# W_up of all experts in one transfer, one low half on GpSimd, and scale two tiles behind, in a conditional adapter kernel on one core

## The reference

```python
h = x @ W_down[e] + b_down[e]        # 512 -> 256
h = gelu(h)                          # exact
h = h @ W_up[e] + b_up[e]            # 256 -> 512
h = x + h
h = (h - mean(h)) * rsqrt(var(h) + 1e-5)
out = h * ln_w[e] + ln_b[e]
```

## Time and profile before

| | |
|---|---|
| time, median of 3 runs | 139.28 us (139.13 to 139.84) |
| profiled execution | 138.9 us, its span 137.1 us |
| PE busy | 126.5 us, 92% of the span |
| DVE busy | 112.4 us, 82% |
| POOL busy | 103.6 us, 76% |
| ACT busy | 84.7 us, 62% |
| TensorE clock granted, mean | 0.992 |
| DMA | 21.94 MB, mean 160 GB/s |

### The profile page before, as it was taken

How to read it: one execution, slowest core, us unless ns; L and a number is a source line. 1 busy time by engine, 2 the same in 40 slices (tenths; PEclk the granted TensorE clock), 3 DMA queues, 4 the chain that set the end, 5 groups by cost and what they waited for, 6 DMA issues and landing times.

```text
span 137.1 us, 4074 instructions
## 1 busy us (share of the span) xinstructions
PE 126.5 (92%) x846; PEld 112.7 (82%) x847; DVE 112.4 (82%) x275; ACT 84.7 (62%) x176; POOL 103.6 (76%) x117
## 2 busy tenths in 40 slices
PE   6969799999979999999999999999999999999830
PEld 6868688878969999999999999999999999998610
DVE  1889669868969979888988897889788978897992
ACT  0587569526696666666676666666666666666600
POOL 7002595567589988888888888888888898889860
PEclk9999999999999999999999999999999999999996
DMA  1964999996463355454444455545546633331355
GB/s 41 329 216 145 268 272 309 292 261 196 143 180 94 116 153 153 155 155 153 153 155 153 153 155 153 153 153 153 153 153 153 153 77 77 81 77 38 86 160 180
DMA packets 13200, 21.94 MB, mean 160 GB/s; under 512 B 2297, under 2 KB 3842, under 8 KB 13186
## 3 DMA queue, kind: packets, MB, share of 16 engines
q1 hardware_dynamic: 8802, 15.74, 40.6%
q10 hardware_dynamic: 4384, 6.05, 14.6%
HBM read 13.39 MB, written 8.65 MB: 161 GB/s over the span
## 4 chain that ended last, share of the span: by engine, by line
PE 67%; DVE 11%; DMA 6%; issue 4%; ACTq 3%; ACT 3%; POOL 3%; DVEq 2%; POOLq 0%
PE hg_ps L896 29%; PE y_ps L924 26%; PE xT_ps L882 8%; DMA wd<-in_L_cond_W_down_dram 4%; PE hg_ps L905 4%; DMA x_sb<-in_x_dram 2%; DVE r_stats L706 2%; DVE hb L694 2%; POOL res L386 2%; DVE xT_lo L686 1%; DVE scaled L727 1%; DVE res L742 1%; DVE gT_lo L700 1%; DVE wu_lo L260 1%; ACTq L457 1%
## 5 line engine op out<-in xcount | busy, mean ns | idle before, releaser
L369 POOL TENSOR_TENSOR xb<-x_sb,bu_rows 128x512 f32<-128x512 f32 x33 | 42.9, 1301 | 11.3 <-DVE bu_rows L681 9.8
L386 POOL TENSOR_TENSOR res<-normed,lnb_rows 128x512 f32<-128x512 f32 x31 | 39.8, 1285 | 12.1 <-ACT normed L488 12.1
L468 ACT ACTIVATE g<-hb 128x256 f32<-128x256 f32 x33 | 13.8, 418 | 35.9 <-DVE hb L694 35.9
L706 DVE BATCH_NORM_STATS2 r_stats<-y_ps 128x6 f32<-128x512 f32 x33 | 22.9, 695 | 7.4 <-issue 7.0
L924 PE MATMUL y_ps<-wu_hi,gT_hi 128*128 x66 | 23.3, 434 | 1.5 <-ACT gT_hi L473 1.4
L896 PE MATMUL hg_ps<-wd_hi,xT_hi 128*128 x132 | 23.8, 302 | 0.9 <-issue 0.8
L686 DVE TENSOR_TENSOR xT_lo<-xT_ps,xT_hi 128x512 fp32r<-128x512 f32 x33 | 22.8, 691 | 1.3 <-ACT xT_hi L463 1.1
L727 DVE SCALAR_TENSOR_TENSOR scaled<-y_ps,r_mv,lnw_rows 128x512 f32<-128x512 f32 x31 | 22.9, 743 | 0.4 <-DMA lnw_rows<-in_L_cond_ln_w_dram 0.4
L375 POOL TENSOR_TENSOR rstd<-var_eps,half_neg 128x1 f32<-128x1 f32 x33 | 18.2, 551 | 5.9 <-DVE var_eps L715 5.8
L488 ACT ACTIVATE normed<-scaled,rstd 128x512 f32<-128x512 f32 x31 | 22.3, 723 | 0.0
L896 PE MATMUL hg_ps<-wd_lo,xT_hi 128*128 x132 | 21.1, 282 | 0.0
(11 more groups left out here) (88 smaller groups left out, 146.8 us busy)
## 6 DMA issues: line engine op xcount, KB each, us to landing
x_sb<-in_x_dram SPq DMA_DIRECT2D x64, 128.0 KB, 2.9
out_dram<-res ACTq DMA_DIRECT2D x33, 128.0 KB, 2.5
out_dram<-res SPq DMA_DIRECT2D x33, 128.0 KB, 2.5
wd<-in_L_cond_W_down_dram ACTq DMA_DIRECT2D x3, 512.0 KB, 5.6
wu<-in_L_cond_W_up_dram SPq DMA_DIRECT2D x3, 512.0 KB, 5.5
lnw_rows<-in_L_cond_ln_w_dram SPq DMA_DIRECT2D x1, 768.0 KB, 9.0
lnb_rows<-in_L_cond_ln_b_dram SPq DMA_DIRECT2D x1, 768.0 KB, 11.0
x_sb<-in_x_dram ACTq DMA_DIRECT2D x2, 128.0 KB, 2.9
```

The source lines that it names most:

```text
L369: pool.tensor_tensor(xb[:, c % DEEP, :], x_sb[:, c % FAR, :], bu_rows[:, ds(e * H, H)], ALU.add).then_inc(xb_ready, 1)
L386: pool.tensor_tensor(res[:, c % FAR, :], normed[:, c % DEEP, :], lnb_rows[:, ds(e * H, H)], ALU.add).then_inc(res_ready, 1)
L706: dve.bn_stats(r_stats[:, c % DEEP, :], y_ps[c % YBANKS][:]).then_inc(stats_ready, 1)
```

## The change

- **Loads.** One static transfer of 1,536 KB holds W_up of all three experts. SP issues it behind the first halves of tiles 0 and 1, and before anything that needs the second part of the tables. The load of 12 registers (L305) is gone; tiles 2 to 6 load their two registers each with `entries` (L276). x of tile 5 now goes behind ln_w.
- **Slots.** wu now lies by expert. ACT, DVE and POOL each load three registers (`wu_from`) that say which expert a slot has, and slice `wu` by them. ACT waits once for the whole transfer.
- **ACT's start.** In tile 0 `gelu(0)` and `seed(1)` now come ahead of `wu_high(0)`.
- **Low halves.** Slots 0 and 1 stay on DVE; slot 2 goes to POOL, behind `add_bias(3)` and ahead of `power(0)`.
- **up.** In tiles 0 to 2 the product with `gT_lo` comes second and that with `wu_lo` last.
- **Distances.** `LATE = 10`: on DVE `scale` runs two tiles behind in 3 to 9, with the catch-up `scale(8)` at the end of 9; on ACT `rescale` runs four behind in 4 to 10, with the catch-up `rescale(7)` at the end of 10, and x_hi(6), which followed x_hi(5) in tile 4, comes in tile 5; on POOL `shift` runs two behind up to tile 9. PE transposes two tiles ahead in 2 to 5, with x of tile 8 as the extra one in tile 5 (before: x of tile 6 in tile 3). The loops start at 6 (PE), 10 (DVE, POOL) and 11 (ACT).

```diff
-        def load_w_up(eng, slot, e):
-            eng.dma_start(wu[:, slot, :, :], w_up[ds(e, 1), :, :].rearrange("a (c p) n -> p (a c) n", p=P)).then_inc(
-                wu_in[slot], 16)
+        def load_w_up(eng):
+            eng.dma_start(wu[:].rearrange("p e c n -> p (e c) n"), w_up.rearrange("e (c p) n -> p (e c) n", p=P)).then_inc(
+                wu_in, 16)
...
+        def w_up_part(source):
+            return wu[:].rearrange("p e c n -> p (e c n)")[:, ds(source * (KB * H), KB * H)]
+
+        def w_up_sources(eng, regs):
+            eng.reg_load(regs, wu_from[0:1, 0:E])
+            return [eng.snap(reg, min_val=0, max_val=E - 1 - slot) + slot for slot, reg in enumerate(regs)]
...
-            sp.wait_ge(slots_ready, 2)
-            sp.reg_load(next_regs, io_table[0:1, 5:17])
-            for t in range(2, 6):
-                if t < 2 + E:
-                    slot = t - 2
-                    load_w_up(sp, slot, sp.snap(next_regs[3 * slot], min_val=0, max_val=E - 1 - slot) + slot)
-                load(t, t, [sp.snap(reg, min_val=0, max_val=B - 1) for reg in next_regs[3 * t - 5:3 * t - 3]])
+            load_w_up(sp)
+            for t in range(2, 5):
+                load(t, t, entries(t, 0, 2))
             sp.dma_start(lnw_rows[:], rows_of(ln_w, P)).then_inc(lnw_in, 16)
-            load(6, 6, entries(6, 0, 2))
+            for t in range(5, 7):
+                load(t, t, entries(t, 0, 2))
...
+            w_up_low(pool, 2, w_up_sources(pool, pool_regs)[2]).then_inc(wu_lo_last, 1)
+            for t in range(LATE):
                 power(t, t)
                 add_bias(t + DEEP, t + DEEP)
+                if t >= 2:
+                    shift(t - 2, t - 2)
+            shift(LATE - 2, LATE - 2)
...
-            wu_high(0)
             gelu(0, 0)
+            seed(1, 1)
+            act.wait_ge(wu_in, 16)
+            wu_high(0, sources[0])
             g_hi(0, 0)
...
+            for t in range(4, LATE + 1):
+                if t == STORE_B_LAG:
+                    act.wait_ge(slots_ready, 3)
+                g_hi(t - 1, t - 1)
+                if t >= STORE_B_LAG:
+                    store(t - STORE_B_LAG, t - STORE_B_LAG)
+                gelu(t, t)
+                if t <= 6:
+                    x_hi(t + 1, t + 1)
+                if t >= 6:
+                    x_hi(t + 2, t + 2)
+                seed(t, t)
+                rescale(t - 4, t - 4)
+            rescale(LATE - 3, LATE - 3)
...
-            w_up_low(dve, 2).then_inc(wu_lo_ready, 1)
...
+            for t in range(3, LATE):
+                stats(t - 1, t - 1)
+                g_lo(t, t)
+                dve.wait_ge(stats_ready, t)
+                down_bias(t + 1, t + 1)
+                mean_var(t - 1, t - 1)
+                variance(t - 1, t - 1)
+                x_lo(t + 2, t + 2)
+                scale(t - 2, t - 2)
+            scale(LATE - 2, LATE - 2)
...
+                if isinstance(t, int) and t < E:
+                    parts = ((gT_hi, wu_hi), (gT_lo, wu_hi), (gT_hi, wu_lo))
...
+            for t in range(2, 6):
+                e_up, e_down = experts_from(t)
+                transpose_g(t, t)
+                down(t + 1, t + 1, e_down)
+                transpose_x(t + 2, t + 2)
+                if t == 5:
+                    transpose_x(t + 3, t + 3)
+                up(t, t, e_up)
```

More of the change, by code:

```diff
@@ L155, in adapter_program @@
         wd_in = [sem(f"wd_in{e}") for e in range(E)]
-        wu_in = [sem(f"wu_in{slot}") for slot in range(E)]
+        wu_in = sem("wu_in")
         biases_in = sem("biases_in")
@@ L404, in _ @@
             add_bias(3, 3)
-            for t in range(3):
+            pool_regs = [pool.alloc_register(f"pool_source{i}") for i in range(E)]
+            w_up_low(pool, 2, w_up_sources(pool, pool_regs)[2]).then_inc(wu_lo_last, 1)
+            for t in range(LATE):
                 power(t, t)
                 add_bias(t + DEEP, t + DEEP)
[L408 to L415, removed]
+                if t >= 2:
+                    shift(t - 2, t - 2)
+            shift(LATE - 2, LATE - 2)
             def body(t, c):
@@ L420, in body @@
                 add_bias(t + DEEP, c + DEEP)
-            for t in range(5, FAR + 1):
-                body(t, t)
-            tiles(pool, body, FAR + 1, TILES - 1 - DEEP)
+            tiles(pool, body, LATE, TILES - 1 - DEEP)
             power(LAST - 2, LAST - 2)
@@ L489, in rescale, with wu_high @@
                                scale=rstd[:, c % DEEP:c % DEEP + 1]).then_inc(normed_ready, 1)
[L491 to L494, removed]
+            def wu_high(slot, source):
+                act.copy(wu_hi[:, slot * KB * H:(slot + 1) * KB * H], w_up_part(source)).then_inc(wu_hi_ready, 1)
             def wd_high(e):
@@ L523, in _ @@
                 keep_up_bias(e)
+            source_regs = [act.alloc_register(f"act_source{i}") for i in range(E)]
+            act.wait_ge(slots_ready, 2)
+            sources = w_up_sources(act, source_regs)
             x_hi(0, 0)
@@ L527, in _ @@
                 keep_down_bias(part)
-            wu_high(0)
             gelu(0, 0)
+            seed(1, 1)
+            act.wait_ge(wu_in, 16)
+            wu_high(0, sources[0])
             g_hi(0, 0)
             x_hi(2, 2)
-            wu_high(1)
+            wu_high(1, sources[1])
             gelu(1, 1)
-            seed(1, 1)
             g_hi(1, 1)
@@ L537, in _ @@
             gelu(2, 2)
-            wu_high(2)
+            wu_high(2, sources[2])
             g_hi(2, 2)
@@ L573, in body @@
                 rescale(t - 3, c - 3)
[L575 to L578, removed]
+            tiles(act, body, LATE + 1, TILES - 3)
             last_places = [place(t) for t in range(TILES - EARLY, TILES)]
@@ L813, in body @@
                 return near[3], near[2]
-            body(5, 5)
-            tiles(dve, body, 6, TILES - 3)
+            tiles(dve, body, LATE, TILES - 3)
             e_last = body(TILES - 2, TILES - 2)
@@ L917, in up @@
                     pe.wait_ge(seeded, t)
-                for n, (g_half, w_half) in enumerate(((gT_hi, wu_hi), (gT_hi, wu_lo), (gT_lo, wu_hi))):
-                    if w_half is wu_lo and isinstance(t, int) and t < E:
+                parts = ((gT_hi, wu_hi), (gT_hi, wu_lo), (gT_lo, wu_hi))
+                if isinstance(t, int) and t < E:
+                    parts = ((gT_hi, wu_hi), (gT_lo, wu_hi), (gT_hi, wu_lo))
+                for n, (g_half, w_half) in enumerate(parts):
+                    if w_half is wu_lo and isinstance(t, int) and t < E - 1:
                         pe.wait_ge(wu_lo_ready, t + 1)
+                    if w_half is wu_lo and isinstance(t, int) and t == E - 1:
+                        pe.wait_ge(wu_lo_last, 1)
                     if g_half is gT_lo:
@@ L954, in _ @@
             up(1, 1, e_up)
[L956 to L969 removed]
+            for t in range(2, 6):
[6 more added lines that the diff above has]
+                up(t, t, e_up)
+            tiles(pe, body, 6, TILES - 4)
             body(TILES - 3, TILES - 3)
```

30 lines of the change are left out of this document (10 added, 20 removed).

## The result

The changed kernel takes 143.12 us (median of four executions; 142.87 to 143.32), beside 139.56 us for the kernel before, whose median now holds a fourth execution of 140.51. The ratio on record is 1.0269, 95% interval 1.0232 to 1.0305 (the two medians alone give 1.0255). That is 3.6 us slower, where 139.9 us had been forecast, in a range to 141.2. Its profiled execution took 142.87 us with a span of 141.1, 4.0 us longer than before. Ratios compare the executions of each kernel that lie within 1.5% of its fastest; two single executions of later kernels, of 181.82 and 698.25 us, are among those left out.

A forecast was written before the change was run, and what follows sets the result against it. PE was taken as the bound from 41.2 us on, so the change could only shift its loop through the ramp and the catch-up: +1.3 - 1.3 + 0.65 = +0.65 us, giving 139.9 us, range 138.3 to 141.2.

The forecast's parts named there:

- term 1: Weights for tiles 0 and 1: the single W_up transfer and a wait at the SBUF port delay up(1), +1.3 us.
- term 2: Tiles 2 to 6: low half off DVE and new distances shorten up(2) to up(6) from 16.38 to 15.06 us, -1.3.
- the landing: Single W_up transfer, issued at 8.6 us, lands at 16.3; bounds 15.1 and 16.7, far end 17.3.
- the port: DVE's low half of slot 0 waits for POOL's add_bias(2) at SBUF: +0.55 us, bounds 0 and 1.3.
- the chain from the cast to up(1): Tile 0's cast, low half, g_lo and up(0) after the landing at 16.3 make up(1) 0.75 us later.
- rival (b): W_up lands late, at 17.3 us: total +1.65 us, 140.9 us; chance 0.21 together with (d).
- (d): W_up transfer starts no earlier, DMA engines still at x of tiles 0 and 1; lands late; 0.21 with rival (b).
- Term 3: Catch-up at tile 10: one more rescale and seed on ACT before g_hi(10) leave PE standing, +0.65 us.
- (a): At the weights' landing: no meeting at the port and a landing by 16.1, total +0.1 us, 139.4 us; chance 0.23.
- (c): Tile 0's delay absorbed, PE at 3.48 us a tile from tile 2: total -1.05 us, 138.2 us; chance 0.18.

The follow-up runs named there:

- the load part alone: The kernel before with only the single static W_up transfer, one wait and register slices, all lists as before: 142.07 us (1.0163); on another chip 143.77 us (1.0330).
- the distances alone: The kernel before with only scale, rescale, shift, x_hi and transposes in their new places; three transfers, all low halves on DVE: 139.26 us, ratio 1.0000.
- the kernel with ACT's start as before: The changed kernel with three W_up transfers behind 12 registers again, and slot 0's cast ahead of gelu(0), seed(1) behind gelu(1): 139.51 us, ratio 1.0024.

## Why the prediction was wrong

The signs of all three terms were right, and the first one was three times too small. What failed is the landing of the single transfer in term 1, and beside it a share of the forecast gain of term 2.

**Term 1, +1.3 forecast, +3.76 measured.** up(1) was put at 22.6 and came at 25.05. The 2.45 us between them are the landing (1.71), the port (0.26) and the chain from the cast to up(1) (0.48).

- The landing. 16.3 was taken from the three W_down transfers, 7.7 us from first issue to last landing, with 17.3 as the far end; the cast was to be at 16.35. The profile has it at 18.06, beyond the far end. The same 1,536 KB needed 7.5 to 9.1 us in ten profiles of kernels with the single transfer behind x of tile 1, and 10.7 in one with x of tile 2 ahead. The prediction had late weights as rival (b), at a chance of 0.21 together with (d), and even (b) stopped at 140.9 us. That a landing is one number was wrong as well: in the three profiles of the changed kernel it took 7.8, 8.7 and 9.1 us, with no change of code.
- The port. 0.55 forecast, 0.81 measured, 1.02 in the 142.56 us execution, nothing in that of 140.65. The step that no row of before showed is shown now: a DVE low half that finds POOL in a sum lasts 2.04 to 2.26 us instead of 1.23, and ends just over a microsecond behind the sum. The Trainium skill ("SBUF — State Buffer", Who interferes with whom) has this as an exclusive lock that the first one keeps; all these profiles agree with it.
- The chain behind the cast. Without the port the forecast has 5.70 us from the cast to up(1) (16.35 to 22.05); the two profiles without it, at full clock, have 6.19 and 6.20. In the first of them gT_lo's product begins 1.75 us behind the end of the cast (1.6 forecast), the last two products of up(0) take 1.21 (1.0 forecast), and from there up(1) needs 2.18 (2.05 forecast). So the 0.75 for a landing at 16.3 was too small in any case.
- x of tile 1, 1.2 us late in the profile. The forecast named traffic of tile 1 as a reason for the weights to be late, but not the reverse. It cost nothing by itself here, as g of tile 0 was ready before the weights.

Why the landing differs from W_down's: W_down had the queues almost alone, and W_up had not, as the windows from issue to landing show (first W_down, kernel before; then W_up, changed kernel; the last number is GB/s).

```profile
1.40:9.10 7.70, 6.51 (x38) 6.03 (x38) 4.61 (x28) 3.88 (x5) 1.70 (x5) 1.00 0.68 216
8.80:17.90 9.10, 6.69 (x51) 5.80 (x49) 5.52 (x8) 5.03 (x10) 2.52 (x2) 1.00 0.94 283
```

That is 1.66 MB in 7.7 us, and 2.58 MB in 9.1, with 1.57 MB of weights in each. The other 1.0 MB in the second is mostly x; 0.79 MB of x (tiles 2, 3 and 4) was queued behind the weights. That this traffic made the landing late is the likely reading, but no run has the transfer without it, so it is not shown.

The half clock was left out too. It is not in the changed kernel's own three profiles, but in one with the same load and the port wait (142.51 us), where it cost 1.52 us, and in the load part alone. Two of the four executions of the result have a mean clock of 0.982 and 0.984, and take 143.32 and 143.29 us, against 0.995 and 0.994 at 142.94 and 142.87; no execution of the kernel before in the later runs is below 0.986. So some of them had it too, as it seems. When it comes is not shown. In the 142.51 us execution PE's idle time was in two pieces (16.85 to 17.70, 19.12 to 19.74), and the clock fell; in the changed kernel's 142.56 us execution the two pieces were longer (1.18 and 1.64 us), and it did not; and of two waits of 2.3 us in one piece, 16.9 to 19.25 and 16.77 to 19.11, the first was followed by half clock and the second by full.

The 140.65 us execution separates the steps by luck: its transfer landed at 16.5, nearly as forecast, and the port cost nothing. There up(2) is still 1.57 us late, up(6) 0.98 and up(10) 1.47, where +1.3, 0 and +0.65 had been forecast. So even with that landing, and with nothing lost at the port, the forecast is short by 0.8 us.

**Term 2, -1.3 forecast, -0.57 measured.** The four intervals are 3.73, 4.35, 4.25 and 3.48, where 3.73, 3.63, 4.22 and 3.48 had been summed. The one that failed is up(3) to up(4): the removed low half was expected to shorten it, and did not. DVE's cycle from down_bias(3) to down_bias(4) is 4.69 us, before 4.70. It consists of the bias, ACT's gelu and x_hi, x_lo, `scale(0)`, the statistics and g_lo, and the low half of slot 2 was never in it, only ahead of it. Even the 0.41 ahead of `scale(0)` is the same. The kernel before has it as a wait for ln_w; but ln_w landed there at about 27.4, when DVE was just done with the piece ahead, and in the changed kernel, where it landed at 23.8, the 0.41 goes to DVE's own sequencer:

```profile
28.52 0.42 DVE L689 TENSOR_TENSOR hb<-hg_ps,bd_rows 128x256 f32<-128x256 f32 x1 [0.65 <-PE hg_ps L883]
...
31.35 0.75 DVE L722 SCALAR_TENSOR_TENSOR scaled<-y_ps,r_mv,lnw_rows 128x512 f32<-128x512 f32 x1 [0.41 <-issue]
...
33.21 0.42 DVE L689 TENSOR_TENSOR hb<-hg_ps,bd_rows 128x256 f32<-128x256 f32 x1 [0.18 <-issue]
```

What the low half's move is worth can be read from two profiles whose weights came alike (cast at 14.89 and 14.90): from up(1) to up(6) the distances alone take 19.64 us, and the kernel with ACT's start as before 19.43, against 19.88 in the kernel before. The second has the low half on POOL and the new order of up's products in addition. So these two win 0.2 us there, where taking out 1.23 us and giving back 0.25 had been reckoned.

**Term 3, +0.65 forecast, +0.52 measured**, at the place and from the wait that were named: the interval to up(10) is 4.00 in place of 3.48 us, and PE's last wait is for ACT's g_hi(10). The distances alone show the same 0.50.

ACT's new start cost what its place says: without the load part the cast stands at 15.90, behind seed(1), and up(1) comes 0.67 late; with the old order it does not. The forecast gave 0.75 for a cast at 16.35; with the 6.07 us from cast to up(1) of that profile it would have been 1.12. Of the rivals, (a) needed a landing by 16.1, and the earliest of a transfer issued at 8.6 to 8.8 was 16.2; (c) needed up(2) to up(6) below 14.7 us, and it took 15.81. (b) names what happened, with a price that was too low.

## What to carry to other kernels

One large transfer in place of three parts makes the part that is needed first wait for the last byte of all. Split it, and give each part its semaphore: with the same bytes queued in the same place that was worth more than half of the loss, in seven of twelve executions. In the other five the data queued behind the weights came late instead, so the order of the queue counts as well. Price a landing from a transfer with the same traffic behind it, not from one that had the queue to itself, and give it a spread. And when a wait of TensorE grows, look at the granted clock after it, in more than one profile.

## What the runs showed of the hardware

- A load of 12 registers from SBUF held SP for 2.50 us; a load of three took 0.69, and with the wait ahead of it 0.9 lay between two issues (slot 0 issued at 9.48, x done at 8.58).
- A VectorE low half (two operands in SBUF, 1.23 us alone) that began 0.1 to 0.3 us behind a GpSimd sum was recorded with 2.04 to 2.26 us, one that began 0.66 behind it with 1.71, and all ended 1.08 to 1.10 us behind the sum. A GpSimd sum of 1.28 us that began together with the low half and was held up by it was recorded with 2.29 and 2.37.
- TensorE's granted clock fell to 0.50 for some 3 us or more in six profiles: in five behind one idle stretch, of 1.84, 2.4, 3.2, 3.5 and 5.8 us, and in one behind pieces of 0.85 and 0.62 us. It stayed at 1.00 behind one stretch of 2.34 us, and behind pieces of 1.18 and 1.64. With matmuls of no use in the gap it stayed at 1.00 in the one profile taken.
- With the same code, half clock made 7.72 us of 6.20 from the cast to up(1).
- The GpSimd low half of 1,024 columns took 2.39 to 2.41 us in every profile, against 1.23 on VectorE; 2.6 had been estimated.
